# Mean aggregation of a graph layer: neighbour weights ahead of the sums, adjacency tiles as stationary operand

## The reference, cut to what matters

```python
def _L3_gnn_ref(x, adj, W_self, b_self, W_nb, b_nb, W_comb, b_comb):
    mask = (adj > 0).astype(x.dtype)
    deg = jnp.sum(mask, axis=1, keepdims=True)
    agg = mask @ x / jnp.maximum(deg, 1.0)
    self_f = x @ W_self + b_self
    nb_f = agg @ W_nb + b_nb
    combined = jnp.concatenate([self_f, nb_f], axis=-1)
    out = combined @ W_comb + b_comb
    return jax.nn.relu(out)
...
    h = jnp.maximum(_layernorm(x, axis=-1), 0.0)
    x = x + _L3_gnn_ref(h, adj, ...)
```

## Time and profile before

| | |
|---|---|
| runs | 2402.12 us median of 3 (2400.92 to 2402.30) |
| profiled execution | 2401.43 us, of which the span of the profile is 2399.7 us |
| TensorE busy | 2103.3 us (88%) |
| VectorE busy | 1979.6 us (82%) |
| ScalarE busy | 1768.2 us (74%) |
| granted TensorE clock, mean | 0.949 |
| last layer | normalisation from 2163 us, mean aggregation from 2207 us, end 2399.7 us |
| loads of the adjacency there | 13 of 832 KB, 4.5 us each to landing; the broadcast of 1/deg 1664 KB |

### The profile page before, as it was taken

How to read it: one execution, slowest core, us unless ns; L and a number is a source line. 1 busy time by engine, 2 the same in 40 slices (tenths; PEclk the granted TensorE clock), 3 DMA queues, 4 the chain that set the end, 5 groups by cost and what they waited for, 6 DMA issues and landing times. The chain is left out here.

```text
span 2399.7 us, 62590 instructions
## 1 busy us (share of the span) xinstructions
PE 2103.3 (88%) x25316; PEld 1713.7 (71%) x25316; DVE 1979.6 (82%) x4384; ACT 1768.2 (74%) x2206; POOL 694.6 (29%) x646
## 2 busy tenths in 40 slices
PE   4647999999957999999978798999998999884999
PEld 3537999999944888888855466666666666554888
DVE  5566999999985988888867799999999999995122
ACT  4546999999975877777754688888888988884000
POOL 0020000000000000000003677778777877860000
PEclk9958999999978999999979799999999999996999
DMA  9787212212102011101007211111111111202222
GB/s 298 278 322 300 91 62 72 81 60 88 58 5 71 22 43 43 43 22 43 23 14 171 93 65 65 66 65 65 65 65 52 50 62 65 65 5 77 71 75 68
DMA packets 78474, 201.08 MB, mean 84 GB/s; under 512 B 26897, under 2 KB 44491, under 8 KB 74745
## 3 DMA queue, kind: packets, MB, share of 16 engines
q1 hardware_dynamic: 77432, 197.27, 24.5%
q10 hardware_dynamic: 768, 0.00, 0.0%
HBM read 161.87 MB, written 26.86 MB: 79 GB/s over the span
## 5 line engine op out<-in xcount | busy, mean ns | idle before, releaser
L1614 DVE CUSTOM_DVE_ANT_0 h_S<-h_ps,h_off 128x832 f32<-128x832 f32 x832 | 800.4, 1019 | 13.9 <-POOL h_off L1476 10.8
L1521 PE MATMUL h_ps<-KS,h_QS 98*128 98x416 f16 x1664 | 442.2, 348 | 99.9 <-DVE h_mx L1614 65.6
L1581 ACT ACTIVATE h_H<-h_S,h_nmx 128x2048 fp8e4<-128x2048 f32 x208 | 416.6, 2003 | 110.5 <-DVE h_nmx L1620 110.5
L834 ACT ACTIVATE b_CA<-b_el,HC 128x1152 fp8e4<-128x1152 f32 (+1 forms) x384 | 435.4, 1219 | 3.2 <-DMA b_el<-el_dram 3.2
L931 PE MATMUL b_pb<-b_x,b_B 128*128 128x132 f16 x5408 | 414.2, 221 | 3.9 <-DVE b_B L896 3.4
L931 PEld LDWEIGHTS b_pb<-b_x,b_B 128*128 128x128 fp8e4 x5408 | 340.3, 96 | 6.6 <-DVE b_B L896 6.2
L1482 POOL TENSOR_SCALAR h_gap<-h_S,h_nmx 128x1280 f32<-128x1280 f32 x208 | 277.1, 1332 | 145.0 <-DVE h_nmx L1620 142.5
L912 PE MATMUL b_pz<-b_x,adjT 128*128 128x134 f16 x2704 | 256.5, 221 | 15.8 <-DMA b_x<-xv_dram 15.8
L1487 POOL TENSOR_SCALAR h_H<-h_gap 128x1280 uint8<-128x1280 f32 x208 | 260.5, 1252 | 17.1
L1552 PEld LDWEIGHTS h_po<-Vhl,h_HT 128*128 128x128 fp8e4 x5408 | 214.8, 98 | 65.0 <-ACT h_HT L1588 0.7
L1245 PE MATMUL c_pd<-c_mv,WnT 128*128 128x256 f16 x2028 | 250.9, 275 | 10.8 <-DMA c_ad<-adjT_dram 10.8
(11 more groups left out here) (208 smaller groups left out, 3300.5 us busy)
## 6 DMA issues: line engine op xcount, KB each, us to landing
h_rows<-in_adj_dram SPq DMA_DIRECT2D x25, 1663.5 KB, 7.7
b_x<-xv_dram SPq DMA_DIRECT2D x48, 435.5 KB, 5.2
s_rows<-in_adj_dram SPq DMA_DIRECT2D x25, 832.0 KB, 6.7
s_rows<-in_adj_dram SPq DMA_DIRECT2D x25, 831.5 KB, 8.1
adjT_dram<-adjT SPq DMA_DIRECT2D x1, 10816.0 KB, 38.0
c_ad<-adjT_dram SPq DMA_DIRECT2D x13, 832.0 KB, 6.1
m_ad<-adjT_dram SPq DMA_DIRECT2D x13, 832.0 KB, 4.5
b_el<-el_dram SPq DMA_DIRECT2D x16, 576.0 KB, 3.8
```

The costliest lines, as they stand in the source:

```text
L834: nc.scalar.activation(dst[:, 0:cols], elr[:, n % 2, 0:cols], ACT.Sigmoid, bias=HC[:, h, 1, jt:jt + 1], scale=STEP, saturate=False).then_i ...
L1521: last = nc.tensor.matmul(ps[:, ch % 2, b, 0:SB], QS[:, i % 2, h, :], KS[:, h, c0:c0 + SB], start=True, stop=True)
L1581: nc.scalar.activation(H[:, g % 2, 0:CA], S[:, g % 2, 0:CA], ACT.Exp, bias=nmx[:, g % 2:g % 2 + 1], scale=1.0, saturate=False).then_inc(s_ ...
L1614: nc.vector.tensor_tensor_reduce(out=two(S[:, g % 2, ch * SW:(ch + 1) * SW]), in0=ps[:, ch % 2, :, 0:SB], in1=two(off[:, i % 2, ch * SW:(c ...
```

## The change

The neighbour weights are applied to h first: P = h @ Mn for each of the 26 tiles, split into float16 parts side by side in `Pn` (512 columns a tile, the parts are the 256 columns each of high and low). The sum of a tile i is then 26 matmuls with a 128 x 128 tile of the adjacency (fp8) as stationary and the 512 columns of `Pn` as moving operand; nodes lie on the partitions. 1/deg becomes a factor per partition and needs no broadcast. `Hn` is not made any more. `neighbour(t)` for three tiles stands ahead of the first sums, and the others between the sums of tile 0. TensorE, ScalarE and VectorE work tile by tile in straight-line code. The diff, cut to its core:

```diff
 def normalise(...)
-            if h_nat is not None:
-                for n, (t0, t1) in enumerate(pieces):
-                    dve.wait_ge(s_hi, nw + len(slots) + 1 + n)
-                    nc.vector.scalar_tensor_tensor(h_nat[:, 1, t0:t1], H[:, t0:t1], HSC, h_nat[:, 0, t0:t1], ALU.mult, ALU.subtract)
...
-            if h_nat is not None:
-                act.wait_ge(s_h, NT)
-                for t0, t1 in pieces:
-                    nc.scalar.activation(h_nat[:, 0, t0:t1], H[:, t0:t1], ACT.Copy, scale=HSC).then_inc(s_hi, 1)
...
 def mean_weights(...)
-        sp.wait_ge(s_rT, 1)
-        sp.dma_start(ideg_dram.rearrange("(t p) -> t p", p=P), dT[:]).then_inc(s_out, 16)
-        sp.wait_ge(s_out, 16)
...
+        dve.wait_ge(s_deg, 2)
+        nc.vector.tensor_scalar(ideg[:], dg[:, 1, :], 1.0 / AGSC, None, ALU.mult)
...
-        pe.wait_ge(s_deg, 2)
-        nc.tensor.transpose(pd[0:NT, 0:P], dg[:, 1, :], k.ident[:]).then_inc(s_tr, 1)
...
-    def scalar_first(act):
-        act.wait_ge(s_tr, 1)
-        nc.scalar.activation(dT[:], pd[0:NT, 0:P], ACT.Copy).then_inc(s_rT, 1)
...
 def mean_aggregate(...)
+    RP, LEAD = 3, 3
+            def load(c):
+                if c >= 2:
+                    sp.wait_ge(s_agg, CT * (c - 1))
...
+            load(0)
+            load(1)
+            for c in range(2, NC):
+                load(c)
+                store(c - 2)
             store(NC - 2)
+            sp.wait_ge(s_x, NT - 1)
             sp.dma_start(out_dram[(NT - 2) * P:(NT - 1) * P, :], k.X[:, NT - 2, :]).then_inc(s_st, 16)
+            sp.wait_ge(s_x, NT)
             for p0, p1 in LAST_CUTS:
...
+        def _(pe):
+            def neighbour(t):
+                if t >= RP:
+                    pe.wait_ge(s_pl, t - RP + 1)
+                for n, (kc, a, b) in enumerate(prods):
+                    last = nc.tensor.matmul(pp[:, t % RP, 0:D], hT[:, a, kc, t * P:(t + 1) * P], m[:, b, 1, kc, :],
+                                            start=(n == 0), stop=(n == len(prods) - 1))
+                last.then_inc(s_p, 1)
+
+            def sums(i):
+                c, q = i // CT, i % 2
+                pe.wait_ge(s_in[c % 2], 16 * (c // 2 + 1))
+                if i >= 2:
+                    pe.wait_ge(s_t, i - 1)
+                for jt in range(NT):
+                    if i == 0:
+                        if jt + LEAD < NT:
+                            neighbour(jt + LEAD)
+                        pe.wait_ge(s_pl, jt + 1)
+                    last = nc.tensor.matmul(pa[:, q, :], ad[:, c % 2, i % CT, jt, :], Pn[:, jt, :], start=(jt == 0), stop=(jt == NT - 1))
+                last.then_inc(s_agg, 1)
+
+            def own(i):
+                if i >= 2:
+                    pe.wait_ge(s_c, i - 1)
+                for n, (kc, a, b) in enumerate(prods):
+                    last = nc.tensor.matmul(po[:, i % 2, 0:D], hT[:, a, kc, i * P:(i + 1) * P], m[:, b, 0, kc, :],
+                                            start=(n == 0), stop=(n == len(prods) - 1))
+                last.then_inc(s_self, 1)
+
+            for t in range(LEAD):
+                neighbour(t)
+            for i in range(NT):
+                sums(i)
+                own(i)
+
+        def _(act):
+            for t in range(NT):
+                act.wait_ge(s_p, t + 1)
+                nc.scalar.activation(Pn[:, t, 0:D], pp[:, t % RP, 0:D], ACT.Copy, scale=AGSC / PSC).then_inc(s_ph, 1)
+            for i in range(NT):
+                act.wait_ge(s_agg, i + 1)
+                if i >= 2:
+                    act.wait_ge(s_t, i - 1)
+                nc.scalar.activation(A[:, i % 2, :], pa[:, i % 2, D:2 * D], ACT.Copy, scale=ideg[:, i:i + 1]).then_inc(s_a, 1)
+
+        def _(dve):
+            for t in range(NT):
+                dve.wait_ge(s_ph, t + 1)
+                nc.vector.scalar_tensor_tensor(Pn[:, t, D:2 * D], pp[:, t % RP, 0:D], AGSC / PSC, Pn[:, t, 0:D],
+                                               ALU.mult, ALU.subtract).then_inc(s_pl, 1)
+            for i in range(NT):
+                q = i % 2
+                dve.wait_ge(s_a, i + 1)
+                nc.vector.scalar_tensor_tensor(B[:, q, :], pa[:, q, 0:D], ideg[:, i:i + 1], A[:, q, :], ALU.mult, ALU.add).then_inc(s_t, 1)
+                dve.wait_ge(s_self, i + 1)
+                nc.vector.scalar_tensor_tensor(R[:, q, 0, :], po[:, q, 0:D], 1.0 / PSC, bias[:], ALU.mult, ALU.add).then_inc(s_c, 1)
+                dve.wait_ge(s_t, i + 1)
+                dve.wait_ge(s_c, i + 1)
+                nc.vector.tensor_tensor(R[:, q, 1, :], R[:, q, 0, :], B[:, q, :], ALU.add).then_inc(s_s3, 1)
+                dve.wait_ge(s_s3, i + 1)
+                nc.vector.scalar_tensor_tensor(k.X[:, i, :], R[:, q, 1, :], 0.0, k.X[:, i, :], ALU.max, ALU.add).then_inc(s_x, 1)
```

More of the change, by code:

```diff
@@ L85, in dram, with normalise @@
         return self.nc.dram_tensor(name, shape, dt, kind="Internal").ap()
-def normalise(k, tag, hT, weights, h_nat=None, also=None):
+def normalise(k, tag, hT, weights, also=None):
     nc = k.nc
@@ L952 @@
 NC = NT // CT
[L955 to L960, removed]
 def cosine_project(k, hT, w, WnT, WHhi, WHlo, rcol, r_dram):
@@ L1656, in layer2, with mean_weights @@
         hard_attend(k, ap["adj"], KS, Vhl, be, q_dram)
-def mean_weights(k, c, ap, m, bias, ideg_dram):
+AGSC = 64.0
+def mean_weights(k, c, ap, m, bias, ideg):
     nc = k.nc
-    s_in, s_tr, s_cp, s_bb, s_mm, s_hi, s_deg, s_rT, s_out, s_b = (
-        k.sem(f"s_w3_{n}") for n in ("in", "tr", "cp", "bb", "mm", "hi", "deg", "rT", "out", "b"))
+    s_in, s_tr, s_cp, s_bb, s_mm, s_hi, s_deg, s_b = (
+        k.sem(f"s_w3_{n}") for n in ("in", "tr", "cp", "bb", "mm", "hi", "deg", "b"))
     raw = k.sb(c, "w3_raw", [P, 2, KC, D], F32)
@@ L1755, in mean_weights, with mean_aggregate @@
     return {"sync": on_sync, "vector_first": vector_first, "vector_mid": vector_mid, "vector_last": vector_last,
-            "scalar_first": scalar_first, "scalar_mid": scalar_mid, "scalar_last": scalar_last,
+            "scalar_mid": scalar_mid, "scalar_last": scalar_last,
             "tensor_first": tensor_first, "tensor_last": tensor_last}
-def mean_aggregate(k, hT, Hn, m, bias, ideg_dram, adjT_dram, out_dram):
+def mean_aggregate(k, hT, m, bias, ideg, adjT_dram, out_dram):
     nc = k.nc
-    s_agg, s_T, s_hi, s_lo, s_mm, s_t, s_x, s_ideg, s_st = (
-        k.sem(f"s_m3_{n}") for n in ("agg", "T", "hi", "lo", "mm", "t", "x", "ideg", "st"))
+    s_p, s_ph, s_pl, s_agg, s_self, s_a, s_t, s_c, s_s3, s_x, s_st = (
+        k.sem(f"s_m3_{n}") for n in ("p", "ph", "pl", "agg", "self", "a", "t", "c", "sum", "x", "st"))
     s_in = [k.sem(f"s_m3_in{i}") for i in range(2)]
     prods = hi_lo_products(KC)
+    RP, LEAD = 3, 3
     with ExitStack() as c:
         ad = k.sb(c, "m3_ad", [P, 2, CT, NT, P], FP8)
[L1769 to L1774, removed]
+        Pn = k.sb(c, "m3_P", [P, NT, 2 * D], F16)
+        A = k.sb(c, "m3_A", [P, 2, D], F32)
+        B = k.sb(c, "m3_B", [P, 2, D], F32)
+        R = k.sb(c, "m3_R", [P, 2, 2, D], F32)
+        pp = k.ps(c, "m3_pp", [P, RP, CH])
+        pa = k.ps(c, "m3_pa", [P, 2, CH])
+        po = k.ps(c, "m3_po", [P, 2, CH])
         block = c.enter_context(nc.Block())
@@ L1778, in _ @@
         def _(sp):
[L1779 to L1782, removed]
-            def store(c):
[L1785 to L1797, removed]
+            def load(c):
+                if c >= 2:
+                    sp.wait_ge(s_agg, CT * (c - 1))
+                sp.dma_start(ad[:, c % 2].rearrange("p t j i -> p t (j i)").bitcast(U8),
+                             adjT_dram[c * CT:(c + 1) * CT].rearrange("t p n -> p t n").bitcast(U8)).then_inc(s_in[c % 2], 16)
+            def store(c):
+                sp.wait_ge(s_x, CT * (c + 1))
+                sp.dma_start(out_dram[c * CW:(c + 1) * CW, :].rearrange("(t p) d -> p t d", p=P),
+                             k.X[:, c * CT:(c + 1) * CT, :]).then_inc(s_st, 16)
+            load(0)
[3 more added lines that the diff above has]
+                store(c - 2)
             store(NC - 2)
-            sp.wait_ge(s_x, NC)
+            sp.wait_ge(s_x, NT - 1)
             sp.dma_start(out_dram[(NT - 2) * P:(NT - 1) * P, :], k.X[:, NT - 2, :]).then_inc(s_st, 16)
+            sp.wait_ge(s_x, NT)
             for p0, p1 in LAST_CUTS:
@@ L1806, in _ @@
         def _(pe):
[L1807 to L1819, removed]
-                last.then_inc(s_agg, 1)
@@ L1851, in _ @@
         @block.vector
         def _(dve):
[L1853 to L1875, removed]
@@ L1897, in build @@
+        normalise(k, "n3", hT, [], also=lambda c1: mean_weights(k, c1, ap, m, bias, ideg))
+        mean_aggregate(k, hT, m, bias, ideg, adjT_dram, out_dram)
 def build(nc, ap, out_dram):
```

24 lines of the change are left out of this document (3 added, 21 removed).

## The result

| | before | after |
|---|---|---|
| runs | 2402.21 us median of 4 (2400.92 to 2403.85) | 2387.52 us median of 4 (2384.56 to 2388.45) |
| profiled execution | 2401.43 us, span 2399.7 | 2387.84 us, span 2386.1 |
| ratio | | 0.9936, 95% interval 0.9921 to 0.9952 |
| layer's first load to VectorE's end of the normalisation | 43.74 us | 34.29 us |
| from there to the end of the span | 192.63 us | 189.22 us |

The kernel is 0.64% faster.

What follows compares the result with a forecast made beforehand. Bound by VectorE's normalisation up to 2207.07 us, 5.11 us to the first sum, then TensorE to the end. Gains 8.0 + 1.96 + 1.7 + 0 + 0.4 make 12.1 us less: 2390.0 us, range 2387.5 to 2394.5.

Steps and rivals of the forecast that it cites:

- part 1: End of the last layer's normalisation: without Hn's copies and subtractions VectorE ends at 2199.1, not 2207.07; gain 8.0 us.
- part 3: Before the first sums: 18 projection matmuls for three tiles hide in the wait for the adjacency load; gain 1.96 us.
- part 4: The sums: 1352 matmuls of 256 columns become 676 of 512 at 215.8 ns each; gain 1.7 us.
- part 5: First tile's sums: the TensorE, ScalarE, VectorE chain of 1.1 us is covered, cost 0; new waits up to 2.6 us.
- part 6: Start of the sums: the fallen clock again loses 1.3 us, as before; bounds 0 to 2.8 us.
- part 7: Kernel's end: two final stores are left, not three, so the tail takes 4.1 us, not 4.55; gain 0.4 us.
- part 2: Degrees: the 1/degree transpose, round trip and broadcast go, one small VectorE operation comes in at the start; taken as 0.
- A: Slower rival: first tile's chain is uncovered, each of 26 steps waits 1.1 us; 2418.6 us, chance 0.03.
- B: Slower rival: short stops hold the clock at half for all of tile 0; 2411 us, chance 0.02.
- C: No-change rival: fetching the loops' straight-line code stalls TensorE and eats the gain; 2402 us, chance 0.05.
- E: Half-gain rival: an unseen wait keeps the normalisation's end from moving by 8 us; 2398 us, chance 0.02.
- D: Larger-gain rival: consecutive 512-column matmuls of the sums overlap in the array; 2317 us, chance 0.01.

Runs made afterwards that it cites:

- one bank: The changed kernel with one bank for the neighbour products and one product ahead, in place of three: 2412.78 us, ratio 1.0043 to the kernel before.
- early loads: The changed kernel with the first two adjacency loads issued in the normalisation, behind the weights' loads: 2387.32 us, ratio 0.9935 to the kernel before.

## Why most parts of the prediction were right, and why its range was wrong

The profiles of three executions before and two after, by stage:

| us | forecast | measured |
|---|---|---|
| Hn gone (part 1) | 8.0 | 8.4; 8.1 where the bias waits for L1718 |
| products beside the load (part 3) | 1.96 | 1.65, with a load 0.2 shorter |
| 676 x 512 columns (part 4) | 1.7 | 1.7, 215.8 ns each |
| first tile's chain (part 5) | 0 | 0.45, one wait at the tile's end |
| loss by the clock (part 6) | 1.3 as before | 1.7; before it was 1.3, 2.3 and 1.4 |
| tail (part 7) | 0.4 | 0.35 |
| normalisation, as it fell out | 8.0 less | 43.74, 42.05, 43.75 against 34.29, 34.47: 8.8 less |
| the stretch behind it | 4.1 less | 192.63, 193.45, 192.49 against 189.22, 189.12: 3.7 less |
| last layer | 12.1 less | 236.37, 235.50, 236.24 against 223.51, 223.59: 12.5 less |

The mechanism of parts 1, 3, 4 and 7 held, and nothing in the traces speaks against part 2's zero, which no run tried alone: the weight products begin 9.4 to 9.7 us after the layer's first load before, and 9.5 and 9.8 after. Part 5 put the chain at nothing, and its reasoning holds only while a neighbour product follows each sum. Behind the last of them the slack is three sums, 0.65 us, against a chain of 1.1: the 0.45 us of the rows above. A wait of TensorE for VectorE in tile 0 was one of the prediction's own signs of being wrong; it was wrong there, by that 0.45 us. The loss by the clock is, in the first profile after, 22.82 us from 2201.74 to 2224.56 against 20.67 at full pace, 2.15, less this wait: 1.7. Part 1 was short by 0.4: it let the bias wait for a product of 2.99 us at half clock (L1738), while after the change the clock rose during L1718, which took 2.49, and nothing waited. Not seen: the 0.17 us by which the block's end became shorter.

Rivals A and B: the slack was there but for the last sum; without it (one bank) the price is 22.4 us, and the short stops do not bring the clock down. C: no stop in the straight-line sums. E: the normalisation's end did move, by 8.4. D: 215.8 ns a matmul of 512 columns. The rule of the Trainium skill (TensorE: Matmul & The Clock Gate, section Back-to-back issue gap) that such a stream takes 131 ns is not borne out by 676 of them; its gap of columns over 2.4 GHz plus 2.5 ns, which the section gives for isolated matmuls, is (215.8 for 512).

**The step that failed** is the last one, "run to run +-0.7" in the range. But for part 5's last wait the mechanism was right; this size was not: of the 14.7 us, 12.9 lie in the last layer of the two profiles (236.37 less 223.51), 0.7 in the layers ahead, which the change doesn't touch, and 1.1 between these profiles and the medians. The second set of the same kernel gave 12.4. Two things were mis-sized. First, the stretch to VectorE's end is not a constant: at half clock the weight products hold ScalarE up, and over all profiles without an edit there it varies by 1.7 to 1.9 us (42.05 to 43.75 before, 33.70 to 35.56 after). I took it from one profile with slow products, and the profile after had faster ones: they ended 1.0 us earlier after the layer's first load (14.45 against 15.50), which with the 0.4 of part 1 is the 1.4 us beyond the 8.0. Second, the layers ahead. The last layer starts at 2163.33, 2166.30 and 2166.76 us before and at 2160.24 to 2166.16 in the changed kernel and its variants, in code that is the same. Layer 0's row of 104 matmuls ahead of layer 1, in the first and the third profile of before and in the one-bank kernel:

```profile
659.59 6.69 PE L931 MATMUL b_pb<-b_x,b_B 128*128 128x132 f16 x104
```

```profile
661.78 6.69 PE L931 MATMUL b_pb<-b_x,b_B 128*128 128x132 f16 x104
```

```profile
656.91 6.69 PE L922 MATMUL b_pb<-b_x,b_B 128*128 128x132 f16 x104
```

So 4.9 us of the spread are there after 657 us already, and the traces have them earlier still: L931's very first matmul starts at 200.1, 201.3 and 196.4 us in these three, and the last of the adjacency loads that layer 0 begins with lands at 180.7, 181.5 and 177.1. TensorE waits for these loads there. What makes them vary was not tried and stays open. The runs of before reach from 2400.11 to 2406.18 us over all sets; the three that I had lay within 1.4. By my estimate from these spreads, an honest range for a median of four such runs had been some 2386 to 2394.

## What to carry to other kernels

When a stage waits on a load, the work that needs no load belongs ahead of the wait, and all of it: three tiles brought 1.65 us, all 26 brought 4.7 more: 2.6 of idle time, 1.7 of the clock's dip that followed it, and 0.45 of a wait at the end of the first tile. A chain that is covered in the steady state has to be priced again where the covering work ends. A difference of a few us in a kernel of 2400 is read from the stage in the trace, not from medians that spread by 6 us, and one profile's duration of a stage that runs at half clock is one draw, not a constant.

## What the runs showed of the hardware that was not expected

Taking work away ahead of a stage can cost part of the gain by the clock, and adding it can give some back. With Hn made, TensorE idled longer, its clock fell early, and it was back at 1.00 when the first tile began (25.81 us from VectorE's end to the first own product); without Hn the clock was still up at the first products, fell at the end of the wait and was at 0.50 for some 3 us of the tile (27.68). Stops of 0.72 us between bursts of 1.04 us, as with one bank, left it at 1.00 throughout. With early loads, a 128 KB broadcast took 5.7 us to land in company of two transfers of 832 KB, and VectorE ended the normalisation 1.4 us later.
